# A graph transformer pair on one core: VectorE's order inside a step is rewritten

## The reference

```
layer 0:  nx = LN(x) * g + b;  q, k, v = nx @ wq + bq, nx @ wk + bk, nx @ wv + bv      (8 heads of 32)
          s  = q k^T / sqrt(32) + (0.1 * adj where adj > 0, else -inf);  a = softmax(s)
          x1 = x + (a v) @ wo + bo
          x2 = x1 + gelu(LN(x1) @ w1 + b1) @ w2 + b2                                   (256 -> 1024 -> 256)
layer 1:  q, k, v from x2;  s = q k^T / sqrt(32), -inf where adj == 0;  a = softmax(s)
          y  = x2 + (a v) @ Wo + bo;   out = LN(y) * gamma + beta
```

## Time and profile before

| what | value |
|---|---|
| time, median of 3 | 2329.34 us (2329.33 to 2329.94) |
| the profiled execution | 2329.64 us, span of its profile 2327.0 us |
| TensorE matmul busy | 2224.4 us, 96% |
| VectorE busy | 1949.8 us, 84% |
| ScalarE busy | 1689.2 us, 73% |
| GpSimd busy | 1140.1 us, 49% |
| granted TensorE clock, mean | 0.985 of full speed |

### The profile page before, as it was taken

One profiled execution on the slowest core, in us unless ns is written; L12 is line 12 of the kernel. 1 busy time (PEld: TensorE's weight loads), 2 busy tenths in 40 slices (PEclk: granted clock), 3 DMA queues, 4 the chain that ended last, 5 costly groups with the idle time before them and its releaser, 6 DMA issues.

```text
span 2327.0 us, 63225 instructions
## 1 busy us (share of the span) xinstructions
PE 2224.4 (96%) x22336; PEld 1918.5 (82%) x22336; DVE 1949.8 (84%) x8684; ACT 1689.2 (73%) x5646; POOL 1140.1 (49%) x1255
## 2 busy tenths in 40 slices
PE   4799999999999999999999999999999999999986
PEld 4688888888888888888888888888888888888875
DVE  4688888888888888888888888888888888888885
ACT  2577777877777877777777777777777777777773
POOL 0245544555544555544555544555544555554454
PEclk8799999999999999999999999999999999999998
DMA  4011100110101111101010100011100011101000
GB/s 116 19 31 31 38 22 26 36 38 31 38 22 29 33 38 31 38 25 33 26 38 31 38 29 29 27 38 31 37 29 29 27 38 32 37 29 30 16 25 16
DMA packets 94326, 76.02 MB, mean 33 GB/s; under 512 B 8128, under 2 KB 93760, under 8 KB 94016
## 3 DMA queue, kind: packets, MB, share of 16 engines
q1 hardware_dynamic: 94016, 71.99, 10.3%
HBM read 55.20 MB, written 16.78 MB: 31 GB/s over the span
## 4 chain that ended last, share of the span: by engine, by line
PE 45%; ACT 26%; DVE 23%; issue 5%; POOL 0%; POOLq 0%; DVEq 0%; ACTq 0%
PE p_bank L1014 36%; ACT scores L575 20%; DVE normed L798 3%; DVE scores L777 3%; PE p_heads L1109 3%; ACT probs_t L606 3%; DVE stats_M L676 2%; PE p_heads L1095 2%; DVE res_a L856 2%; DVE x_two L690 2%; PE p_bank L1129 2%; PE p_bank L1033 2%; DVE stats_C L676 1%; DVE res_c L856 1%; DVE moments_M L681 1%
## 5 line engine op out<-in xcount | busy, mean ns | idle before, releaser
L575 ACT ACTIVATE scores<-scores,negmax 128x128 f32<-128x128 f32 x2048 | 795.3, 392 | 107.5 <-DVE negmax L777 107.1
L522 POOL TENSOR_TENSOR scores<-scores,inverse 128x512 f32<-128x512 f32 x512 | 543.9, 1067 | 632.5 <-DVE inverse L787 632.5
L575 ACT ACTIVATION_READ_ACCUMULATOR scores<-scores,negmax 128x1 f32 x2048 | 389.3, 190 | 0.0
L1014 PE MATMUL p_bank<-w_down,hidden 128*128 128x256 f32 x3072 | 381.3, 284 | 0.0
L1014 PEld LDWEIGHTS p_bank<-w_down,hidden 128*128 128x128 f32 x3072 | 374.2, 190 | 8.6 <-issue 5.9
L1014 PE MATMUL p_bank<-normed,w_up 128*128 128x512 f32 x1536 | 368.5, 396 | 1.2 <-DVE normed L798 1.1
L1014 PEld LDWEIGHTS p_bank<-normed,w_up 128*128 128x128 f32 x1536 | 283.7, 188 | 66.1 <-issue 7.1
L1109 PE MATMUL p_heads<-ident,scores 128*128 128x128 f32 x2048 | 315.7, 278 | 18.1 <-DVE negmax L777 17.6
L1109 PEld LDWEIGHTS p_heads<-ident,scores 128*128 128x128 f32 x2048 | 237.1, 142 | 52.0 <-DVE negmax L777 41.2
L597 ACT ACTIVATE p_bank<-p_bank,ready_cols 128x512 f32<-128x512 f32 x256 | 169.5, 662 | 130.1 <-PE p_bank L1014 124.5
L1014 PE MATMUL p_bank<-w_o,heads_t 128*128 128x256 f32 x1536 | 248.2, 297 | 3.1 <-DVE heads_t L845 3.1
(11 more groups left out here) (113 smaller groups left out, 3811.9 us busy)
## 6 DMA issues: line engine op xcount, KB each, us to landing
x_in<-in_x SPq DMA_DIRECT2D x32, 512.0 KB, 3.9
res_a<-in_x SPq DMA_DIRECT2D x32, 512.0 KB, 4.1
out<-res_c SPq DMA_DIRECT2D x128, 128.0 KB, 1.8
adj_a<-in_adj SPq DMA_DIRECT2D x32, 256.0 KB, 2.9
adj_c<-in_adj SPq DMA_DIRECT2D x32, 256.0 KB, 2.8
res_c<-in_L_gnn_w SPq DMA_DIRECT2D x1, 512.0 KB, 5.9
values_c<-in_L_gnn_w SPq DMA_DIRECT2D x1, 512.0 KB, 6.7
piece_room<-in_L_gnn_w SPq DMA_DIRECT2D x1, 512.0 KB, 7.8
```

The source lines that it names most:

```text
L522: nc.gpsimd.tensor_tensor(rows_c, rows_c, inverse[:, k % 2, heads].unsqueeze(2).broadcast_to([P, HC, P]), ALU.mult).then_inc(probs_made, 1)
L575: last = nc.scalar.activation(scores[:, k % 2, h], scores[:, k % 2, h], ACT.Exp, scale=-1.0, bias=negmax[:, k % 2, h:h + 1], accum_out=tot ...
L1014: last = nc.tensor.matmul(dst, stationary(i), moving(j), start=(n == 0), stop=(n == total_n - 1))
```

## The change

VectorE's order inside a step, and nothing else. add_residual is split in two: the addition itself, and `measure`, the statistics. The addition, the statistics, and then the normalisations of list late now stand ahead of the invert of heads 4 to 7. The normalisations therefore come behind the turned copy and the evacuations of early and mid. One of them does not: that of unit A3 (`closing`, in step 2), after which the MLP's transposes can begin, comes right behind the masks, ahead of the evacuation of the step before's fill. In step 4 the ahead operation (XT of C) is evacuated between the addition and the statistics; in the other steps it stays where it was, behind the invert. In step 3 the normalisation no longer stands ahead of the evacuation of UP 0. What SyncE, GpSimd, TensorE and ScalarE issue, and in which order, is as before.

```diff
             def add_residual(t, r):
 
                 _, stage, b = t.unit(r)
-                group = t.group(r)
                 bank, number = t.bank(("W", r))
                 dve.wait_ge(filled[bank], number)
-                dve.wait_ge(biased[stage], group * 2 + b // 2 + 1)
+                dve.wait_ge(biased[stage], t.group(r) * 2 + b // 2 + 1)
                 x = residual[stage]
                 nc.vector.tensor_tensor(x[:, b, :], p_bank[bank][:, 0:D], x[:, b, :], ALU.add
                                         ).then_inc(drained[bank], 1)
+
+            def measure(t, r):
+
+                _, stage, b = t.unit(r)
+                bank, number = t.bank(("W", r))
                 dve.wait_ge(drained[bank], number)
-                layer_norm_steps("M" if stage == "A" else "C", x, b, b + 1, (group * GB + b) * 3)
+                layer_norm_steps("M" if stage == "A" else "C", residual[stage], b, b + 1, (t.group(r) * GB + b) * 3)
...
                     if k in s.units:
                         mask_scores(t, k, 1)
+                    closing = [r for r in s.late.get(k, []) if t.unit(r)[1:] == ("A", GB - 1)]
+                    for r in closing:
+                        apply_norm(t, r)
                     for op in s.fill.get(k - 1, []):
                         if op[0] in ("Q", "K"):
                             evacuate(t, op)
                     if k in s.units and k != s.behind:
                         invert(t, k, 0)
-                    for r in s.late.get(k, []):
-                        apply_norm(t, r)
                     for op in s.early.get(k, []) + s.mid.get(k, []):
                         if op[0] == "DOWN":
                             prepare(t, k)
...
                     for op in s.early.get(k, []) + s.mid.get(k, []):
                         if op[0] not in ("DOWN", "UP"):
                             evacuate(t, op)
+                    for _, r in only("W", lag):
+                        add_residual(t, r)
+                    if k == 4:
+                        for op in s.ahead.get(k, []):
+                            evacuate(t, op)
+                    for _, r in only("W", lag):
+                        measure(t, r)
+                    for r in s.late.get(k, []):
+                        if r not in closing:
+                            apply_norm(t, r)
                     if k in s.units and k != s.behind:
                         invert(t, k, 1)
-                    for _, r in only("W", lag):
-                        add_residual(t, r)
-                    for op in s.ahead.get(k, []):
-                        evacuate(t, op)
+                    if k != 4:
+                        for op in s.ahead.get(k, []):
+                            evacuate(t, op)
...
                             if op == "W":
                                 add_residual(t, r)
+                                measure(t, r)
```

## The result

The changed kernel takes 2338.32 us (median of 6 runs, 2336.54 to 2342.02) against 2329.32 us for the kernel before (6 runs). The ratio is 1.0043, 95% interval 1.0031 to 1.0056. The forecast was 2308 us and faster, so the direction was wrong; 2338 also lies 2 us above the range.

A forecast was written before the change was run, and what follows sets the result against it. Six steps outside the MLP stall TensorE 2.1 us a turn, mostly through the ScalarE-VectorE chain. Step-by-step gains of 0.65 us x 30 turns = 19.5, plus 2 for other turns: 2329.6 - 21.5 = 2308 us; range 2284 to 2336.

The forecast's parts named there:

- (b): VectorE's probability copy ahead of the normalisations: nothing waits for the copy; step 0's two normalisations cost 0.65 instead of 1.45 us.
- The fifth, step 6: Of five late normalisations, four find GpSimd idle; step 6's meets the bias additions as before, 0.64 us.
- (e): Cover for later reciprocals: step 4's moves 2.9 us, delaying GpSimd's finish and res_a's load; step 6's residual waits some 0.2.
- The rule quoted there: A two-port-mode instruction and a GpSimd one exclude each other, the later blocking; each late normalisation could pay 0.75 us.
- The sign that was to be watched: Turn 0 or the residual waiting on GpSimd's probabilities or bias over 0.5 us a turn would mean slower.
- (a): Residual and statistics, 1.18 us, move into VectorE's hole before the second reciprocal; the ScalarE chain's floor falls 6.12 to 4.9.
- (c): Step 4, XT evacuated ahead of the statistics: K projection starts 0.40 earlier, step 5's masks 0.55 later, a loss of 0.55.
- (d): Step 2, closing normalisation first: 0.3 ahead of the bank's evacuation, the transposes start about 0.1 us sooner.
- The rival on the slower side: Step 5's masks 0.55 late, carried through the turn, step 0 wins nothing back: 17 us, 2346 us; chance 0.14.
- Its own mark: The slower outcome is decided if step 0's masks start no earlier than 1050.79, their start in the kernel before.
- the prediction's clock: New times in the forecast are written on the clock of the turn 1027 to 1069 us.
- The rival of TensorE's floor: All six holes outside the MLP close, to 37.6 us a turn: 65 us, 2265 us; below 2290 chance 0.12.

The follow-up runs named there:

- e5: The changed kernel with GpSimd adding stage A's bias to one column of each half only; 2311.5 us.
- e6: The changed kernel with step 6's normalisation alone in its old place, behind the first reciprocal and ahead of the turned copy; 2346.2 us.
- e13: The changed kernel with rstd ahead of finish, res_a loaded ahead of the second store, and stage A's bias behind step 5's first probabilities; 2344.5 us.
- e7: The kernel before with only residual and statistics moved ahead of the second reciprocal; 2308.6 us.
- e11: e7 with step 0's two normalisations late, behind the statistics; 2316.1 us.
- e3: The changed kernel with step 4 wholly in the order of before, the other seven steps in the new one; 2322.2 us.
- e10: e7 with the closing normalisation right behind the masks in step 2; 2307.9 us.
- e1: The changed kernel with step 4's second reciprocal ahead of the residual again; 2338.7 us.
- e12: e7 with rstd ahead of finish on GpSimd in every step; 2282.5 us.
- e9: e12 with stage A's bias behind step 5's first probabilities, and the load of res_a ahead of the second store; 2279.7 us.

## Why the prediction was wrong

The step that failed is in part (b): "The fifth, step 6, meets the bias additions as it does today (0.64 us)", and with it the step time of 7.04 for step 7. It is 7.75. Of the 0.95 us a turn between forecast (39.12 for the six steps) and measurement (40.07), 0.71 is step 7, 0.15 step 2, 0.06 step 6, and 0.03 the other three; 0.95 x 30 = 28 us, and 2308 + 28 = 2336. The rest is step 3, where 0.05 was to be won and 0.02 was lost.

The term that was mis-sized is the length of step 6's normalisation. The text says 0.64, and the sum holds less: its residual at 1042.1 and its masks at 1043.81 are 1.71 apart, of which residual and statistics take 1.21 (1045.71 - 1044.50 in the changed kernel) and the reciprocal 0.10 (1046.80 - 1046.70), so 0.40 is left for the normalisation. In the changed kernel it is 0.99 (1046.70 - 1045.71), 0.59 more. e5 showed that the 0.71 is GpSimd's: with the bias work gone step 7 is even 0.2 under the forecast (6.85). I had followed (e)'s chain on GpSimd for the residual's sake (forecast a wait of some 0.2, measured 0.15) and had the bias additions end at about the moment at which the normalisation comes, but did not ask what GpSimd does next without a hole: probabilities, 1.04 us. The rule quoted there, of the Trainium skill's page "SBUF — State Buffer", section "Who interferes with whom", was the right one, and the traces agree with it each time: 1.07 us in the changed kernel, 1.37 in e6, 1.50 in e13, against 0.41 in the changed kernel's step 5 and in e5, where GpSimd is idle. It was weighed against a timeline that had shifted. The sign that was to be watched, a wait of over 0.5 us of turn 0 or the residual, could not show it: the loss stands in no wait of these two but in the length of an instruction.

Point by point:

- (a) Residual and statistics first: the mechanism was right. The reciprocal's wait fell from 113.6 to 28.5. Its worth was never priced by itself; e7 gives 21 us, the size of the whole forecast. That e7 lands on 2308 is luck, as two of its steps differ from the forecast's by 0.4 us and more.
- (b) Copy first, normalisations late: the copy's wait fell from 15.5 to 5.3, and the two of step 0 did take 0.74 instead of 1.45. But as a gain it was wrong: e11 shows step 0's late normalisations to cost 7.5 us once (a) is in. A normalisation ahead of the copy fills the time in which VectorE waits for turn 1 anyhow. The forecast's own sum had step 1 at 6.34 and so had the loss in it; the text calls it a gain "given back". The late normalisations, step 4's apart, and the closing one together cost 13.6 us: e3, which has them, takes 2322.2, and e7, which has neither, 2308.6.
- (c) Step 4: forecast 0.55 later masks, 6.95 for step 5; measured 0.58 and 6.96. What followed was not "made good by step 0": e3 shows the 0.55 to be lost in full, 16 us. TensorE's gain in steps 6 and 0 is there with and without it. So against 2329.3 the account is 21 won by (a), some 14 lost by (b) and (d), 16 lost by (c): 9 slower.
- (d) Closing: forecast 0.1; e10 shows nothing beyond the noise.
- (e) Of the cover: turn 1 never waited for probabilities; the residual waited 0.15. That the lateness comes from step 4's reciprocal was wrong (e1); it is step 5's second one that releases the chain in step 6.
- The rival on the slower side had the right sign. Its own mark came true: the masks of step 0 start at 1053.22, which is 1050.93 on the prediction's clock (step 5's scores at 1029.07), no earlier than 1050.79. It was right that step 4's loss is carried (e3), and wrong that nothing is won back: steps 6 and 0 are 0.81 shorter. The rest of the loss is step 7's 0.74, which no rival had.
- The rival of TensorE's floor (2265, under 2290 with chance 0.12) was put aside because VectorE is nearly as busy as a step is long. e12 and e9 come to 2282.5 and 2279.7 with the same work on VectorE; their six steps take 38.07 against the floor of 37.6.

Stays open: what makes step 2 last 6.99 in the changed kernel and 6.83 in e11, which has only step 0's normalisations late (the 0.15 of the 0.95); and why step 1 is 0.14 longer in e12 than in e7. No run took either apart.

## What to carry to other kernels

An instruction's cost in a new place is the state of its neighbours there, in the new schedule: follow each queue that shares something with it to the operation after the one it meets. A late instruction isn't free because nobody waits for its result; it is free if its engine has a hole there, and moving step 0's two out of a hole cost 7.5 of the 21 us that (a) had won. When an instruction is held in each place of its own engine's queue that was tried, as step 6's normalisation was, move the other engine's chain: rstd ahead of finish on GpSimd gave 26 us on top of e7, the best order of VectorE alone. But look first whether that chain has room: in e13 the same move, with the bias early, only carried the hold to another step.

## What was not expected of the hardware

A step's length repeats to 0.01 to 0.05 us over nearly all full turns of every kernel, so that a table of steps from one profile shows in which step a difference of 0.1% (0.08 us a turn) lies. And VectorE's normalisation of 128 x 256 values stretches from 0.38 to as much as 1.50 us beside GpSimd's tensor operations, while GpSimd's own probabilities, when they meet one, went from 1.04 to 1.14 us.
